# A recurrent kernel: the reset gate of one more step in eight summed over two halves, and one piece of work moved behind another

## The chip, the cores and the metric

The kernel runs on one core of one Trainium2 chip. The metric is the device time of one execution in microseconds. Before the change it is 1040.35 us, the median of three runs (1040.12 to 1040.90).

## The reference

64 sequences of 128 steps and 512 features go through a GRU whose first state is `cond_1024`; the result is added to x. After every fourth step, but not after the last, the state also goes through a propagation layer:

```python
comb = jnp.concatenate([x_t, h], axis=-1)
z = jax.nn.sigmoid(comb @ Wz + bz)
r = jax.nn.sigmoid(comb @ Wr + br)
comb2 = jnp.concatenate([x_t, r * h], axis=-1)
h_cand = jnp.tanh(comb2 @ Wh + bh)
h_new = (1.0 - z) * h + z * h_cand
h_next = jnp.where(prop, jnp.tanh(h_new @ Wp + bp), h_new)
```

All inputs are float32. Each step depends on the one before.

## The kernel before

**Layout.** Features lie on the 128 partitions in KC = 4 groups, the 64 sequences along the free dimension. The 128 steps are cut into 16 blocks of BLOCK = 8. `t` is the step, `m` its block and `s = t % 8` its place in the block. Every float32 operand of a matmul is split into two float16 parts, hi and lo, and a product is made of three of them: lo weights by hi values, hi by hi, hi weights by lo values.

**Two kinds of matmul.** The recurrent products (of h, of q = r*h, and of the state to propagate) have 64 columns. A *joint* product (`rec_both`, L1365 to L1371) multiplies the hi weights with the hi and lo values in one matmul of 128 columns; the two halves of the accumulator have to be added afterwards by VectorE (`tensor_reduce`, L1049 for R in two halves, L1067 for Z, L1084 for C), and the accumulator is opened (seeded) in both halves with half of the value (`seed`, L615). Steps 19 to 108 are joint for the update gate Z. The reset gate R is joint in them at places 0 to 6, not at place 7. The candidate C is joint at places 1, 4 and 6.

**The part of x.** The products of x with the input weights don't depend on h. They are made one or more blocks ahead and kept in `x_part`, from which the accumulators are seeded. For blocks 2 to 14 (`SEVEN`) the product of each gate is made of seven products of 2 x 2 quarters instead of eight: 21 *groups* a block, numbered 0 to 20 in `ORDER`, each 12 matmuls of 256 columns in one bank of PSUM. `STAGES_AT` says at which place TensorE makes which: at place 3 groups 7 and 8 ahead of the propagation and 9 behind it, at place 6 groups 15, 16 and 17, at place 7 groups 18 and 19 ahead of the propagation and 20 behind it. In a step with a joint R, the first four matmuls of the step's first group are put between Z and C (`AHEAD_OF_C`, L1413).

**Ends.** Most groups are read out by ScalarE (`read_stage`, L555). Products 5 and 6 of a gate (groups 4, 5, 11, 12, 17 and 19) are read by VectorE: `end_quarter` (L958 to L971) multiplies the bank and adds it to a quarter of `x_part` that ScalarE has begun. Group 17 is product 5 of the candidate, group 19 product 6. Before, the end of a group was issued in the step in which TensorE makes the group, the last thing of VectorE there but for the propagation. Group 20, product 7 of the candidate, goes into the bank of group 19, and so TensorE waits for its end:

```python
                elif product == 6:
                    pe.wait_ge(c12_begun, 2 * count)
                else:
                    pe.wait_ge(c22_out, count)
```

Group 9 (place 3) is product 3 of Z and waits for `first_copied` alone.

**The order of a step**, which is written out by hand for each engine. TensorE: R, Z (with the last of R's parts in between), the four matmuls ahead, C, then the groups of x, at places 3 and 7 the propagation between them. VectorE: R's reductions, q in hi (L1054) and in full (L1056), its lo part (L1032), Z's reduction (L1067), a split of x (L896), at joint candidates their reductions, keep (L1088), new (L1108), the state in hi (L1117), in full (L1120) and lo (L1032), at places 3 and 7 `add_states` for one step (L1127 by way of L1037), sums of quarters of x (L956), the ends (L969), and at places 3 and 7 the propagated state (L1147, L1150, L1032) and `add_states` for the other three. ScalarE: sigmoid of R, a split of x, squares, sigmoid of Z, tanh of C, the seeds of R and Z for the next step, the read-outs of x, the tanh of the propagation, the seed of C.

Of the kernel before, what the change touches and what calls it, by code (L numbers as in the profile page):

```python
# [16 lines left out]
BLOCK = 8  # L17
# [15 lines left out]
AHEAD = 32  # L33
REC_SUM_AT = 4
EARLY_PROP_SHARE = 1.4
JOINT_RESET_AT = (0, 1, 2, 3, 4, 5, 6)
AHEAD_OF_C = 4
JOINT = range(19, 109)
JOINT_CANDIDATE_AT = (1, 4, 6)
WITHIN_C = 4  # L40
SQUARES_AT = (0, 1, 2, 3)
# [7 lines left out]
SEVEN = range(2, 15)  # L49
# [4 lines left out]
ORDER = [(0, 1), (0, 2), (0, 3), (0, 4), (0, 5), (0, 6), (1, 1), (0, 7), (1, 2), (1, 3), (1, 4), (1, 5), (1, 6),  # L54
         (2, 1), (2, 2), (1, 7), (2, 3), (2, 5), (2, 4), (2, 6), (2, 7)]

STAGES_AT = [((), (0, 1)), ((), (2, 3, 4)), ((), (5, 6)), ((7, 8), (9,)), ((), (10, 11, 12)), ((), (13, 14)), ((), (15, 16, 17)), ((18, 19), (20,))]

SLOT_AT = {2: (5, 6, 6, 7, 8, 9, 10), 3: (4, 5, 6, 7, 7, 8, 9)}
SLOT_AT_LATER = (1, 2, 3, 4, 5, 6, 7)  # L60
# [8 lines left out]

def gru_kernel(nc, x, h0, wz, wr, wh, wp, biases, out):  # L70
    BLOCKS, _, KC, _, B = x.shape
    H = wp.shape[0]
    D = wr.shape[0] - H
# [22 lines left out]
    def in_tail(steps):  # L96

        if steps > len(TAIL_SHARES):
            return PER_GROUP * len(TAIL)
        shared = TAIL[:-KC]  # L100
        columns = [PER_GROUP * (of.stop - of.start) for _, _, of in shared]
        share, count = sum(columns) * sum(TAIL_SHARES[:max(steps, 0)]) / sum(TAIL_SHARES), 0
        for group in columns:
            count += min(int(max(share, 0) * PER_GROUP / group + 0.001), PER_GROUP)
            share -= group
        return count
# [30 lines left out]
    def stages_of(t):  # L137

        m, s = divmod(t, BLOCK)
        return STAGES_AT[s] if m + 1 in SEVEN else ((), ())  # L140

# [38 lines left out]
    with ExitStack() as ctx:  # L180
# [186 lines left out]
        def propagates(t):  # L367
            return t % CHUNK == CHUNK - 1 and t < T - 1

        def joint(t):  # L370

            return t in JOINT

        def behind_propagation(t):

            return propagates(t) and joint(t) and joint(t + 1)

        def joint_reset(t):

            return joint(t) and t % BLOCK in JOINT_RESET_AT  # L380

        def joint_candidate(t):

            return joint(t) and t % BLOCK in JOINT_CANDIDATE_AT

        def resets_before(t):
            return sum(joint_reset(step) for step in range(t))

        def candidates_before(t):
            return sum(joint_candidate(step) for step in range(t))  # L390

        def begun(t, n, stages):

            if n != stages[0] or not joint_reset(t):
                return 0
            return AHEAD_OF_C + (WITHIN_C if joint_candidate(t) else 0)
# [106 lines left out]
        def _(act):  # L503
# [81 lines left out]
            def squash_sums(g, func, summed, count, halves):  # L585

                for n, half in enumerate(halves):
                    act.wait_ge(summed, count + n + 1)
                    nc.scalar.activation(gate[g][:, half], gate[g][:, half], func, scale=unscale[:, g:g + 1]).then_inc(gate_ready[g], 1)  # L589
# [116 lines left out]
            for t in range(T):  # L706
# [25 lines left out]
                if joint(t):  # L732
                    squash_sums(Z, ACT.Sigmoid, update_summed, JOINT.index(t), WHOLE)
                else:
# [13 lines left out]
                if t + 1 < T and not ahead:  # L748
                    for g in (R, Z):
                        if g not in late and not (g == Z and behind_propagation(t)):  # L750
                            seed(g, t + 1)
# [10 lines left out]
                if propagates(t):  # L762
                    for n in range(first, middle):
                        copy_group(n)
                        seed_behind(n, late, t + 1)
                    for n in stages_first:
                        read_stage(m + 1, n)
                    act.wait_ge(squares_ready, KC + squares_before(t))
                    squash(PROP, ACT.Tanh, props_before(t), HALVES)
                    if behind_propagation(t):  # L770
                        seed(Z, t + 1)
                    for n in range(middle, last):
                        copy_group(n)
                        seed_behind(n, late, t + 1)
                    for n in stages_last:
                        read_stage(m + 1, n)
                else:
                    for n in range(first, last):
                        copy_group(n)
                        seed_behind(n, late, t + 1)  # L780
                    for n in stages_last:
                        read_stage(m + 1, n)
# [6 lines left out]
        def _(dve):  # L789
# [27 lines left out]
            def make_scale(col):  # L817

                one = slice(col, col + 1)
                dve.wait_ge(mag_reduced[col], 1)  # L820
                if col in ROOTS:
                    root_powers(pow2[:, one], scale[:, one], mag_sum(col), ROOTS[col], pow2_ready[col], 1, scale_ready[col])
                else:
                    powers(pow2[:, one], scale[:, one], mag_sum(col), pow2_ready[col], scale_ready[col])
                dve.wait_ge(pow2_ready[col], 1)
                if col < HS:
                    nc.vector.tensor_scalar(unscale[:, one], pow2[:, one], h_unscale, 0.5, ALU.mult, ALU.mult).then_inc(unscale_ready[col], 1)
                    dve.wait_ge(scale_ready[col], 1)
                    nc.vector.tensor_scalar(seed_scale[:, one], scale[:, one], h_scale, None, ALU.mult).then_inc(seed_scale_ready[col], 1)
                else:  # L830
                    nc.vector.tensor_scalar(unscale[:, one], pow2[:, one], 0.5, None, ALU.mult).then_inc(unscale_ready[col], 1)
                    if col > HS:
                        dve.wait_ge(unscale_ready[col], 1)
                        nc.vector.tensor_scalar(part_unscale[:, 0, col - WIN:col - WIN + 1], unscale[:, one], x_pow2[:, 0:1], 0.5,
                                                ALU.mult, ALU.mult).then_inc(part_unscale_ready, 1)
# [49 lines left out]
            def split_x(m, k, count=1):  # L885

                dve.wait_ge(x_scale_ready, m + 1)
                dve.wait_ge(x_hi_ready[m % 2], x_splits(m) - KC + k + count)
                nc.vector.scalar_tensor_tensor(out=x_lo[m % 2][:, k:k + count, :], in0=x_blk[m % RING][:, k:k + count].rearrange("p k s b -> p k (s b)"),  # L889
                                               scalar=x_scale[:, m % 2:m % 2 + 1], in1=x_hi[m % 2][:, k:k + count, :],  # L890
                                               op0=ALU.mult, op1=ALU.subtract).then_inc(x_lo_ready[m % 2], count)
# [66 lines left out]
            def end_quarter(m, n):  # L958

                g, product = ORDER[n]  # L960
                if product == 5:
                    dve.wait_ge(c12_begun, 2 * sevens(m, g))
                    bank, jh, done = BANK_C, 0, c12_out
                else:
                    dve.wait_ge(c22_begun, 2 * sevens(m, g))
                    bank, jh, done = BANK_A[g], 1, c22_out
                dve.wait_ge(seven_summed, len(ORDER) * (m - SEVEN.start) + n + 1)
                dve.wait_ge(part_unscale_ready, GATES + m)
                nc.vector.scalar_tensor_tensor(out=part_quarter(m, g, jh, 1), in0=in_halves(x_acc[bank][:]),  # L969
                                               scalar=part_unscale[:, m % 2, g:g + 1], in1=part_quarter(m, g, jh, 1),  # L970
                                               op0=ALU.mult, op1=ALU.add).then_inc(done, 1)  # L971
# [68 lines left out]
            for t in range(T):  # L1040
                m, s = divmod(t, BLOCK)
# [34 lines left out]
                if t == 1:  # L1076
                    make_scale(PROP)
                if t == JOINT[0] - 2:
                    nc.vector.tensor_scalar(half_seed_scale[:], seed_scale[:, R:C + 1], 0.5, None, ALU.mult).then_inc(half_seed_scale_ready, 1)
# [56 lines left out]
                if m + 2 == LAST:  # L1136
                    for k in SPLIT_AT.get(s, ()):
                        split_x(m + 2, k)
                for n in stages_of(t)[0] + stages_of(t)[1]:
                    if ORDER[n][1] in (5, 6):  # L1140
                        end_quarter(m + 1, n)
                if t in (1, 2):
                    split_rec(PROP, t - 1)
# [366 lines left out]
```

## Time and profile before

| | us |
|---|---|
| median of 3 runs | 1040.35 |
| the profiled execution | 1040.76 |
| its span | 1038.90 |
| TensorE busy | 1033.4 (99%) |
| VectorE busy | 880.9 (85%) |
| ScalarE busy | 777.0 (75%) |

The span runs from the first to the last instruction of the trace. PE is the matmuls of TensorE, PEld its weight loads, DVE is VectorE, ACT is ScalarE. Matmuls overlap: one of 64 columns is shown with 194 ns, though the next begins long before; what counts is the distance from start to start. The granted clock is full over the whole table of slices. `[0.16 <-DVE x_part L969]` behind an instruction says that its engine was idle for 0.16 us before it and that the named instruction released it; `issue` stands for no releaser that the trace shows.

### The profile page before, as it was taken

Reading aid. Unit: us, or ns where it says so; the run is one execution under the profiler, and the core shown is the slowest. Engines: PE = TensorE matmul, PEld = TensorE weight load, DVE = VectorE, ACT = ScalarE, POOL = GpSimd, SP = SyncE. Lnnn points to the kernel's source line nnn. Section 1 sums busy time; section 2 is a strip of 40 time slices with the busy share of each in tenths; the row PEclk is TensorE's granted clock in tenths of the full one; section 3 lists DMA queues with packets and bytes.
Section 4 is the critical chain, followed back from the end, with each engine's and each line's share of the span. In section 5 each row is a group of like instructions: output and inputs, shape, how many; then the busy total and the mean of one; then the engine's idle time right before and its main releaser. Section 6 shows DMA issues by size and latency. Waiting matters only on the chain.

```text
span 1038.9 us, 48087 instructions
## 1 busy us (share of the span) xinstructions
PE 1033.4 (99%) x20746; PEld 953.2 (92%) x20746; DVE 880.9 (85%) x2880; ACT 777.0 (75%) x1789; POOL 0.2 (0%) x4
## 2 busy tenths in 40 slices
PE   9999999999999999999999999999999999999998
PEld 4577999999999999999999999999999999999998
DVE  6978888898989899898989989989898998876666
ACT  6877777777878778777887777878777777665565
POOL 0000000000000000000000000000000000000000
PEclk9999999999999999999999999999999999999999
DMA  9312211001111011110011110111100100000001
GB/s 331 110 43 84 84 54 44 23 23 43 43 43 43 4 44 42 44 43 23 23 44 43 44 43 11 35 44 43 44 29 17 43 23 23 23 10 17 24 24 44
DMA packets 38484, 47.26 MB, mean 45 GB/s; under 512 B 2176, under 2 KB 34048, under 8 KB 37888
## 3 DMA queue, kind: packets, MB, share of 16 engines
q1 hardware_dynamic: 38000, 44.12, 12.6%
q8 instruction: 163, 2.67, 1.1%
q14 instruction: 49, 0.40, 0.1%
q10 hardware_dynamic: 272, 0.07, 0.0%
HBM read 27.40 MB, written 16.78 MB: 43 GB/s over the span
## 4 chain that ended last, share of the span: by engine, by line
PE 98%; DMA 1%; SPq 0%; DVE 0%; issue 0%; ACT 0%; DVEq 0%
PE acc L1360 38%; PE x_acc L1274 34%; PE acc L1368 17%; PE x_acc L1164 8%; DMA x_part<-wz_dram 1%; PE x_acc L1295 0%; SPq L419 0%; SPq L416 0%; DVE mag_win L982 0%; SPq L425 0%; SPq L424 0%; DVE x_lo L889 0%; PE acc L1170 0%; ACT gate L745 0%; DVE new L1099 0%
## 5 line engine op out<-in xcount | busy, mean ns | idle before, releaser
L1274 PE MATMUL x_acc<-x_hi,win_hi 128*128 128x256 f16 x1092 | 298.0, 273 | 0.0
L1274 PE MATMUL x_acc<-x_lo,win_hi 128*128 128x256 f16 x1092 | 297.9, 273 | 0.0
L1274 PE MATMUL x_acc<-x_hi,win_lo 128*128 128x256 f16 x1092 | 297.9, 273 | 0.0
L589 ACT ACTIVATE gate<-gate,unscale 128x128 f32<-128x128 f32 (+1 forms) x316 | 128.6, 432 | 136.4 <-DVE gate L1067 77.7
L595 ACT ACTIVATE gate<-acc,unscale 128x128 f32<-128x128 f32 (+1 forms) x384 | 123.8, 371 | 97.9 <-PE acc L1360 97.7
L1368 PE MATMUL acc<-h_split,wrec_hi 128*128 128x128 f16 x2704 | 178.8, 220 | 0.0
L1360 PE MATMUL acc<-h_split,wrec_lo 128*128 128x64 f16 x4096 | 177.5, 194 | 0.0
L1360 PE MATMUL acc<-q_split,wrec_hi 128*128 128x64 f16 x4000 | 162.2, 194 | 0.0
L555 ACT ACTIVATE x_part<-x_acc,bias,part_unscale 128x256 f32<-128x256 f32 x312 | 154.6, 561 | 6.4 <-PE x_acc L1274 5.5
L1360 PEld LDWEIGHTS acc<-h_split,wrec_lo 128*128 128x128 f16 x4096 | 154.2, 98 | 4.7
L1368 PEld LDWEIGHTS acc<-h_split,wrec_hi 128*128 128x128 f16 x2704 | 153.7, 98 | 0.0
L1360 PEld LDWEIGHTS acc<-q_split,wrec_hi 128*128 128x128 f16 x4000 | 136.5, 98 | 0.1
L617 ACT ACTIVATE acc<-x_part,half_seed_scale 128x512 f32<-128x512 f32 x203 | 135.3, 686 | 0.0
L1360 PE MATMUL acc<-q_split,wrec_lo 128*128 128x64 f16 x2544 | 120.8, 194 | 0.0
L1360 PE MATMUL acc<-h_split,wrec_hi 128*128 128x64 f16 x2784 | 117.6, 194 | 0.0
L1274 PEld LDWEIGHTS x_acc<-x_hi,win_lo 128*128 128x128 f16 x1092 | 106.8, 98 | 11.2
L1274 PEld LDWEIGHTS x_acc<-x_hi,win_hi 128*128 128x128 f16 x1092 | 106.8, 98 | 10.9 <-DVE x_part L969 0.2
L1274 PEld LDWEIGHTS x_acc<-x_lo,win_hi 128*128 128x128 f16 x1092 | 106.8, 98 | 10.0
L1360 PEld LDWEIGHTS acc<-q_split,wrec_lo 128*128 128x128 f16 x2544 | 98.6, 98 | 6.0 <-issue 0.5
L1360 PEld LDWEIGHTS acc<-h_split,wrec_hi 128*128 128x128 f16 x2784 | 96.4, 98 | 0.0
L1054 DVE TENSOR_TENSOR q_split<-gate,h_ring 128x128 f16<-128x128 f32 x192 | 54.8, 292 | 46.4 <-ACT gate L595 36.5
L626 ACT ACTIVATE acc<-x_part,seed_scale 128x256 f32<-128x256 f32 x180 | 83.0, 477 | 2.1 <-ACT x_part L522 0.4
(141 smaller groups left out, 1517.5 us busy)
## 6 DMA issues: line engine op xcount, KB each, us to landing
out_dram<-x_blk SPq DMA_DIRECT2D x30, 512.0 KB, 3.2
x_blk<-x_dram SPq DMA_DIRECT2D x24, 512.0 KB, 3.8
x_blk<-x_dram SPq DMA_DIRECT2D x3, 1024.0 KB, 8.7
x_part<-wz_dram SPq DMA_DIRECT2D x4, 256.0 KB, 6.8
x_part<-wh_dram SPq DMA_DIRECT2D x4, 256.0 KB, 6.6
x_part<-wr_dram SPq DMA_DIRECT2D x1, 1024.0 KB, 10.9
x_part<-wz_dram SPq DMA_DIRECT2D x1, 1024.0 KB, 13.1
x_part<-wh_dram SPq DMA_DIRECT2D x1, 1024.0 KB, 15.3
```

The lines of the kernel that those rows point to most:

```text
L555: nc.scalar.activation(part_quarter(m, g, jh, nh)[:, j], in_halves(x_acc[bank][:])[:, j], ACT.Identity, bias=bias[:, g, 2 * jh + j:2 * jh ...
L589: nc.scalar.activation(gate[g][:, half], gate[g][:, half], func, scale=unscale[:, g:g + 1]).then_inc(gate_ready[g], 1)
L595: nc.scalar.activation(gate[g][:, half, :], acc[g][:, half, :], func, scale=unscale[:, g:g + 1]).then_inc(gate_ready[g], 1)
L617: nc.scalar.activation(acc_bank[g][:], added.unsqueeze(1).broadcast_to([P, 2, KC, B]), ACT.Copy, scale=half_seed_scale[:, g:g + 1]).then_i ...
L626: nc.scalar.activation(acc[g], added, ACT.Copy, scale=seed_scale[:, g:g + 1]).then_inc(seed_ready[g], 1)
L1054: nc.vector.tensor_tensor(q_split[:, half, 0, :], gate[R][:, half, :], h_in[:, half, :], ALU.mult).then_inc(q_hi_ready, 1)
L1164: return nc.tensor.matmul(x_acc[bank][:, 0:cols], weights[g][:, 2 * (j // 2) + k // 2, k % 2, j % 2 * P:(j % 2 + 1) * P], values[m % 2][:, ...
L1274: mm = nc.tensor.matmul(in_halves(x_acc[bank][:])[:, j], weights[g][:, slot_w, k, j * P:(j + 1) * P], in_halves(values[m % 2][:, slot_x, : ...
L1360: mm = nc.tensor.matmul(bank[:, j, :], weights[g][:, k, j * P:(j + 1) * P], values[:, k, lo, :], start=False, stop=False, skip_group_check ...
L1368: mm = nc.tensor.matmul(acc_bank[g][:, :, j, :], wrec_hi[g][:, k, j * P:(j + 1) * P], values[:, k], start=False, stop=False, skip_group_ch ...
```

## The change

R becomes joint in all steps from 19 to 108, place 7 included (11 steps: 23, 31, ..., 103). With it come, in those steps: 16 matmuls of 128 columns in place of 32 of 64, two reductions on VectorE, a seed of both halves in the step before on ScalarE, and the first four matmuls of group 18 ahead of C. The conditions of C and of the seed behind the propagation are written anew and pick the same steps as before. The end of group 17 moves from place 6 to place 7, behind that of group 19, in all 13 blocks that make groups; the other ends stay where they were.

```diff
-JOINT_RESET_AT = (0, 1, 2, 3, 4, 5, 6)
 AHEAD_OF_C = 4
-JOINT = range(19, 109)
+JOINT_RESET = range(19, 109)
+JOINT = JOINT_RESET
...
+ENDS_AT = [(), (4,), (5,), (), (11, 12), (), (), (19, 17)]
...
         def behind_propagation(t):
 
-            return propagates(t) and joint(t) and joint(t + 1)
+            return propagates(t) and t + 1 in JOINT_RESET
 
         def joint_reset(t):
 
-            return joint(t) and t % BLOCK in JOINT_RESET_AT
+            return t in JOINT_RESET
 
         def joint_candidate(t):
 
-            return joint(t) and t % BLOCK in JOINT_CANDIDATE_AT
+            return t in JOINT_RESET and t % BLOCK in JOINT_CANDIDATE_AT
...
-                for n in stages_of(t)[0] + stages_of(t)[1]:
-                    if ORDER[n][1] in (5, 6):
+                if m + 1 in SEVEN:
+                    for n in ENDS_AT[s]:
                         end_quarter(m + 1, n)
```

## Rows read from the trace of the kernel before

**Rows 1.** The page: busy time of TensorE (part 1), chain that ended last (part 4).

```profile
PE 1033.4 (99%) x20746; PEld 953.2 (92%) x20746; DVE 880.9 (85%) x2880; ACT 777.0 (75%) x1789; POOL 0.2 (0%) x4
...
PE 98%; DMA 1%; SPq 0%; DVE 0%; issue 0%; ACT 0%; DVEq 0%
```

**Rows 2.** Windows, TensorE, the 11 steps of place 7: stretch, length, busy.

```profile
415.49:425.20 9.71, 9.67 (x215) 1.00 0.02 5
...
542.14:551.63 9.49, 9.49 (x215) 1.00 0.02 3
...
794.99:804.71 9.72, 9.72 (x215) 1.00 0.01 3
...
sum 104.83, PE 104.79; mean PE 9.53
```

**Rows 3.** Windows, TensorE, one step of place 3 (step 59).

```profile
509.93:519.38 9.45, 9.45 (x199) 1.00 0.01 2
```

**Rows 4.** Timeline, TensorE, start of that step: start, duration, instruction.

```profile
509.93 0.86 PE L1360 MATMUL acc<-h_split,wrec_lo 128*128 128x64 f16 x24
510.63 1.06 PE L1368 MATMUL acc<-h_split,wrec_hi 128*128 128x128 f16 x16
511.52 0.40 PE L1360 MATMUL acc<-h_split,wrec_lo 128*128 128x64 f16 x8
...
513.08 0.40 PE L1360 MATMUL acc<-q_split,wrec_lo 128*128 128x64 f16 x8
```

**Rows 5.** Timeline, TensorE, place 7 of the same block: the candidate begins.

```profile
544.90 0.40 PE L1360 MATMUL acc<-q_split,wrec_lo 128*128 128x64 f16 x8
```

**Rows 6.** Timeline, VectorE, the same step of place 7.

```profile
543.46 0.75 DVE L969 SCALAR_TENSOR_TENSOR x_part<-x_acc,part_unscale,x_part 128x512 f32<-128x512 f32 x1 [1.22 <-ACT x_part L555]
...
548.99 0.48 DVE L1037 SCALAR_TENSOR_TENSOR x_blk<-h_ring,unscale,x_blk 128x256 f32<-128x256 f32 x1
549.38 0.75 DVE L969 SCALAR_TENSOR_TENSOR x_part<-x_acc,part_unscale,x_part 128x512 f32<-128x512 f32 x1
550.98 0.54 DVE L1147 TENSOR_SCALAR h_split<-gate,scale 128x128 f16<-128x128 f32 x2 [0.85 <-ACT gate L595]
```

**Rows 7.** Timeline, VectorE, the step of place 3.

```profile
511.72 0.76 DVE L1049 TENSOR_REDUCE gate<-acc 128x128 f32<-128x256 f32 x2 [0.42 <-PE acc L1368]
...
517.30 0.48 DVE L1037 SCALAR_TENSOR_TENSOR x_blk<-h_ring,unscale,x_blk 128x256 f32<-128x256 f32 x1
517.70 0.69 DVE L956 TENSOR_TENSOR sum_b<-x_blk,sum_b 128x512 f32<-128x512 f32 x1
```

**Rows 8.** Timeline, VectorE, the step of place 7 from 415.49.

```profile
422.47 0.29 DVE L1032 TENSOR_TENSOR q_split<-h_ring,q_split 128x128 f16<-128x128 f32 x1 [0.25 <-issue]
...
423.08 0.74 DVE L969 SCALAR_TENSOR_TENSOR x_part<-x_acc,part_unscale,x_part 128x512 f32<-128x512 f32 x1
```

**Rows 9.** Timeline, weight loads of TensorE, the same step: group 20 begins.

```profile
423.87 0.10 PEld L1274 LDWEIGHTS x_acc<-x_hi,win_hi 128*128 128x128 f16 x1 [0.16 <-DVE x_part L969]
```

**Rows 10.** Timeline, VectorE, the step of place 7 from 794.99.

```profile
802.58 0.75 DVE L969 SCALAR_TENSOR_TENSOR x_part<-x_acc,part_unscale,x_part 128x512 f32<-128x512 f32 x1
```

**Rows 11.** The page's seeds (whole span), and ScalarE's timeline at places 7 and 3.

```profile
L617 ACT ACTIVATE acc<-x_part,half_seed_scale 128x512 f32<-128x512 f32 x203 | 135.3, 686 | 0.0
...
L626 ACT ACTIVATE acc<-x_part,seed_scale 128x256 f32<-128x256 f32 x180 | 83.0, 477 | 2.1 <-ACT x_part L522 0.4
...
543.32 0.48 ACT L626 ACTIVATE acc<-x_part,seed_scale 128x256 f32<-128x256 f32 x1
...
512.18 0.73 ACT L589 ACTIVATE gate<-gate,unscale 128x128 f32<-128x128 f32 x2 [1.09 <-DVE gate L1049]
```

**Rows 12.** Timeline, VectorE: two ends in a row (place 4's), and place 0.

```profile
274.33 1.40 DVE L969 SCALAR_TENSOR_TENSOR x_part<-x_acc,part_unscale,x_part 128x512 f32<-128x512 f32 x2
...
553.42 0.76 DVE L1049 TENSOR_REDUCE gate<-acc 128x128 f32<-128x256 f32 x2 [0.17 <-PE acc L1368]
```

**Rows 13.** Timeline, VectorE, step 111, behind the end of group 19.

```profile
930.95 0.54 DVE L1147 TENSOR_SCALAR h_split<-gate,scale 128x128 f16<-128x128 f32 x2 [1.05 <-ACT gate L595]
```

## The prediction

> **What bounds the kernel now.** I read the page first: its table of busy time and its chain of waits say the same thing, TensorE is busy for 99% of the span and the chain that ended last lies on it for 98% [rows 1]. So an edit is worth what it does to the time between TensorE's instructions, and nothing else. Next I took TensorE's busy time in stretches that are one time step each. Steps are called by their place in the block of 8 (step 23, 31, ..., 103 are the 11 steps of place 7 between 19 and 108, the only ones whose reset gate changes). Nine of the 11 take 9.49 us, two take 9.71 and 9.72, and all together 104.83 [rows 2]. A step of place 3 is built in the same way (it propagates too, and multiplies three groups of 12 for the next block), and its reset gate is already joint: the usual one takes 9.45 us, with 16 matmuls fewer [rows 3]. Place 3 is the model of what place 7 becomes.
>
> In the order of time, TensorE at place 3 goes from one group to the next without a gap, at 0.70 / 24 = 29 ns for a matmul of 64 columns and 0.89 / 16 = 56 ns for one of 128 [rows 4]. One joint matmul replaces two plain ones: 2 x 29.2 - 55.6 = about 2.5 ns each, 0.04 us for 16, which is 9.49 - 9.45. So TensorE gains next to nothing from joining: the columns stay, only instructions go.
>
> **What the joint reset gate does to VectorE.** Its own price is on VectorE and ScalarE: the two halves of the sum must be added before the sigmoid, so q is late, and with it everything behind q. At place 7 the candidate's first matmul begins 544.90 - 542.14 = 2.76 us into the step [rows 5, 2]; at place 3 it is 513.08 - 509.93 = 3.15 us [rows 4]. TensorE fills this with the first four matmuls of the step's first group (18, which the change now begins there), so it does not stop. VectorE has no such filling; from q on it runs its instructions one behind the other, and the delay is kept to the end. At place 7 it adds the step's result to x (L1037) at 548.99 - 542.14 = 6.85 us into the step and begins the end of quarter 19 (L969) at 7.24 [rows 6]; at place 3 the same L1037 begins at 517.30 - 509.93 = 7.37 and what is behind it at 7.77 [rows 7]. Place 7 gets the list of place 3 on VectorE up to that point (two reductions, q, its two parts, the update gate's reduction, one split of x, keep, new, the two forms of h, L1037), so the end of quarter 19 will begin at 7.77 instead of 7.24: 0.53 us later.
>
> **Who waits for it.** Product 7 of the candidate (group 20, the last of the step) goes into the bank that the end of quarter 19 reads, and TensorE waits for c22_out before it. Place 3 has no such wait: its last group, 9, needs only ScalarE's copy of group 6, made long before. The trace of before shows the wait at work once in a way that can be measured. In the step from 415.49 VectorE had an idle piece of 0.25 us that the trace puts down to nothing but issue, the end of quarter 19 began at 423.08, that is 7.59 into the step [rows 8], TensorE's weight load for group 20 came 0.16 us late with that very instruction as its releaser [rows 9], and the step ended at 425.20, 2.12 us after the beginning of the end of quarter 19. The second long step repeats it: 802.58 to 804.71 is 2.13 us [rows 10, 2]. In the nine other steps 7.24 + 2.12 = 9.36, which is 0.13 us ahead of 9.49: that is all the slack there is. The long step is late by 0.35 at the end of quarter 19 and by 0.22 at its own end, again 0.13 apart.
>
> So a step of place 7 after the change lasts 7.77 + 2.12 = 9.89 us. Eleven of them: 108.79, against 104.83 now. **The sum is +3.96 us.** Of this 9 x 0.40 = 3.6 come from the ordinary steps and 0.36 from the two long ones, which lose less because they are late already.
>
> **The rest of the change.** The end of quarter 17 leaves place 6, where VectorE waited for ScalarE's copy (L555) and only began at 543.46, 1.32 us into place 7 [rows 6]. Kept there with a joint gate, and later by the 0.21 of R's larger seed on ScalarE, it would free VectorE at 1.32 + 0.21 + 0.66 = 2.19, and the reductions are due at 511.72 - 509.93 = 1.79 [rows 7]: q would be late by 0.4. Moved, it holds up nothing there. Behind 19 it starts 0.66 us after it (two ends in a row take 1.40 together, one alone 0.74, so the second starts 0.66 behind the first [rows 12]), at 8.43, and the propagated state (L1147) follows at 9.09 instead of 550.98 - 542.14 = 8.84. Its first half is written 0.29 later, at 9.38. The next step begins at 9.89, so this is hidden by the wait before group 20; were that wait gone, 9.38 plus the passing of the semaphore would be at the step's very end (9.45) and could cost up to 0.1 us a step. VectorE is then free at 553.25 + 0.25, 11.36 into the step; its next reduction had 0.17 us of idle time [rows 12] and is itself moved on by 0.40, so nothing is passed on. Whoever waits for c12_out does so in the next block, several us later. Steps 15 and 111 get only the move: at 111 VectorE sat idle for 1.05 us before L1147 [rows 13], against 0.66 for one more end, so I take nothing for them (a loss of up to 0.1, no gain).
>
> ScalarE: the seed of R before place 7 becomes one of 512 elements, 686 ns instead of 477 [rows 11]. Its seed of C ends at 543.80, would end at about 544.03, 1.89 us into the step, and the joint sigmoid is due at 512.18 - 509.93 = 2.25 [rows 11]. Slack 0.36, cost nothing. If it were gone, q would be late and TensorE would stand before C.
>
> **Bounds.** The unknown in the sum is VectorE's pieces of 0.25 to 0.35 us of idle time without a releaser. In the steps of before two of 11 had one ahead of the end of quarter 19; there was then 0.13 us to take it, now there is none, so each costs its 0.35 in full. The change adds 22 reductions, so where they fall is open: none gives +3.96, one +4.3, two +4.6, four +5.4. Downwards: were the 0.04 us that each step saves on TensorE not met at all by the wait (all 11 steps at 9.45), the sum would be 103.95 - 104.83 = -0.9. I take one piece, as the count lies between none and two: +4.3, or 4.15 with the slight chance of none weighed in. The span of the profiled execution is 1038.90 of its 1040.76 us; the 1.86 around it stay. It lies 0.4 above the median of the runs, 1040.35, to which the difference is added: 1044.5.
>
> **The rivals.** (1) The wait is not felt, the other side: VectorE gets to the end of quarter 19 by 7.33 us into the step (9.45 - 2.12), the point from which it decides. Then the steps take 9.45 and the kernel 1040.35 - 0.9 = 1039.5, within 0.2% of before. For it speaks that TensorE at place 3 never stops; against it that place 3 has no group that waits for an end, and that every instruction between q and that end is already back to back. (2) The end of quarter 19 is early enough but 17 behind it delays h: up to 0.1 us in 11 steps less the 0.04 saved, 1041. It needs (1) first. (3) ScalarE is not free at 2.25: q late by, say, 0.5 (the seed's 0.21 and a piece of idle time), which adds to the end of quarter 19: 11 x 0.5 more, about 1050. The measured 0.36 speaks against it. (4) Loading weights sets TensorE's pace, and 16 loads fewer a step is the true gain: a load lasts 0.10 us [rows 9], 16 x 0.10 = 1.6 us a step, 17.6 in all, 1023. Against it: loads that follow at 29 ns each, and 9.49 against 9.45 with those 16 gone.
>
> The Trainium skill has a rule that speaks for (4): "TensorE: Matmul & The Clock Gate", sections "Back-to-back issue gap" and "LDWEIGHTS (loading the stationary operand)", says that in a stream of load and matmul the spacing is set by both, 81 ns at 128 columns, and that a load takes its columns over 1.2, 107 ns for 128. By 107 ns a load the change would save 16 x 107 x 11 = 18.8 us. The trace does not agree, with 56 ns at 128 columns and 29 at 64; it agrees with the formula that the page calls the isolated gap.
>
> **How the numbers follow.** Forecast 0.84; (1) 0.08, (2) 0.03, (3) 0.04, (4) 0.01. About 2.1 us (0.2%) is what a measurement of this kernel can tell from no change. The forecast and (3) are slower by more: 0.88. (1) and (2) are within: 0.11. (4) is faster: 0.01. The range for 8 in 10 holds the forecast with none to four pieces of idle time (1044.3 to 1045.7), and 0.9 below and 0.4 above for the small terms and for runs: 1043.4 to 1046.1.
>
> **What would show it.** In the profile after: TensorE's weight load of L1274 with L969 of VectorE as releaser in every step of place 7, about 0.4 us each; steps 23, 31, ... of 9.89 us; the end of quarter 19 at 7.77 into the step and 17 at 8.43; the candidate's first matmul at 3.15; the steps of place 0 to 6 unchanged (9.45 at place 3). It is wrong if place 7 takes 9.45 (rival 1), or if TensorE stops before the candidate's matmuls (rival 3).

## The result, and the profile after

Six runs of the changed kernel have a median of 1045.07 us (1044.3 to 1045.5), against 1040.7 for the kernel before beside them: a ratio of 1.0041, 95% interval 1.0029 to 1.0054. It is 4.4 us slower. The forecast was 1044.5, range 1043.4 to 1046.1.

The windows of TensorE over the 11 steps of place 7, stretch, length and busy time, which answer to [rows 2]. Three of the 11 rows of the kernel after, a usual one between the two long ones, and their sum:

```profile
416.78:426.80 10.02, 9.63 (x199) 1.00 0.02 5
...
544.14:554.03 9.89, 9.62 (x198) 1.00 0.01 2
...
862.35:872.49 10.14, 9.73 (x198) 1.00 0.02 4
sum 109.19, PE 105.98; mean PE 9.63
```

Nine steps take 9.89 or 9.90 us where nine took 9.49, and in each TensorE is shown idle for 0.27 us, which it was not before. (What it lost is more. The step would be 9.45 long without the stop, as experiment 8 shows, so the stop is 0.44. The shown gap is shorter, since a matmul of 64 columns is shown with 194 ns though the next can begin 29 ns behind it.) The sum is 4.36 above the 104.83 of before. The span grew by 4.5, from 1038.9 to 1043.4, so these 11 steps hold nearly all of it. The execution as a whole took 1045.23.

The same place as in [rows 6], in the step from 544.14, on VectorE (start, duration, instruction, idle time before it). The lines of the code are one higher than before (L970 is the end of a quarter, L1038 the addition to x, L1148 the propagated state):

```profile
545.93 0.75 DVE L1050 TENSOR_REDUCE gate<-acc 128x128 f32<-128x256 f32 x2 [1.69 <-PE acc L1369]
...
551.51 0.48 DVE L1038 SCALAR_TENSOR_TENSOR x_blk<-h_ring,unscale,x_blk 128x256 f32<-128x256 f32 x1
551.91 1.40 DVE L970 SCALAR_TENSOR_TENSOR x_part<-x_acc,part_unscale,x_part 128x512 f32<-128x512 f32 x2
553.23 0.47 DVE L1148 TENSOR_SCALAR h_split<-gate,scale 128x128 f16<-128x128 f32 x2
...
555.82 0.76 DVE L1050 TENSOR_REDUCE gate<-acc 128x128 f32<-128x256 f32 x2 [0.40 <-PE acc L1369]
```

TensorE in that step, where the candidate begins, and its weight load for group 20, which answers to [rows 9]:

```profile
547.30 0.40 PE L1361 MATMUL acc<-q_split,wrec_lo 128*128 128x64 f16 x8
```

```profile
552.71 0.10 PEld L1275 LDWEIGHTS x_acc<-x_hi,win_hi 128*128 128x128 f16 x1 [0.39 <-DVE x_part L970]
```

The waits of the changed kernel between 225 and 872.6 us (who waited for whom: us in total, times, longest) name the wait in all 11 steps. Before, the first of the two rows stood there once, with 0.2, and the second not at all:

```profile
PEld x_acc L1275 <- DVE x_part L970: 4.5, 11, 0.5
PE x_acc L1275 <- DVE x_part L970: 3.2, 11, 0.4
```

And the chain that ended last, part 4 of the page, which was 98% TensorE in [rows 1], now goes through VectorE:

```profile
PE 92%; DVE 6%; ACT 1%; issue 1%; DVEq 0%
```

6% of the span is some 60 us, while the loss is 4.4. In the step from 544.14 the chain leaves TensorE at the reductions (545.93) and comes back to it at the load for group 20 (552.71). So it counts all of VectorE's work that leads up to the late end, with two sigmoids of ScalarE, and most of it ran beside a busy TensorE. The share says where to look, the windows say how much.

### The profile page after: what moved, and what is told of

Its sections match the earlier page's. It is cut to its first block, busy times and chain, and to the rows that moved or that the text cites. A ratio compares the mean times of both kernels' runs of the same rounds, so it can differ in the third digit from the quotient of the medians.

```text
span 1043.4 us, 47768 instructions
## 1 busy us (share of the span) xinstructions
PE 1035.2 (99%) x20570; PEld 953.9 (91%) x20570; DVE 887.2 (85%) x2902; ACT 780.6 (75%) x1789; POOL 0.2 (0%) x4
## 4 chain that ended last, share of the span: by engine, by line
PE 92%; DVE 6%; ACT 1%; issue 1%; DVEq 0%
PE acc L1361 33%; PE x_acc L1275 32%; PE acc L1369 17%; PE x_acc L1165 8%; PE x_acc L1296 1%; ACT gate L590 1%; DVE q_split L1033 1%; DVE x_part L970 1%; DVE x_lo L897 1%; DVE gate L1068 1%; DVE q_split L1118 1%; DVE x_blk L1038 0%; DVE gate L1050 0%; DVE keep L1089 0%; DVE new L1109 0%
## 5 line engine op out<-in xcount | busy, mean ns | idle before, releaser
L590 ACT ACTIVATE gate<-gate,unscale 128x128 f32<-128x128 f32 (+1 forms) x338 | 136.6, 430 | 140.5 <-DVE gate L1068 78.1
L1369 PE MATMUL acc<-h_split,wrec_hi 128*128 128x128 f16 x2880 | 190.3, 219 | 0.0
L596 ACT ACTIVATE gate<-acc,unscale 128x128 f32<-128x128 f32 (+1 forms) x362 | 117.0, 372 | 90.0 <-PE acc L1361 90.0
L1361 PE MATMUL acc<-h_split,wrec_lo 128*128 128x64 f16 x4096 | 173.7, 193 | 0.0
L1369 PEld LDWEIGHTS acc<-h_split,wrec_hi 128*128 128x128 f16 x2880 | 163.7, 98 | 0.0
L618 ACT ACTIVATE acc<-x_part,half_seed_scale 128x512 f32<-128x512 f32 x214 | 142.1, 686 | 0.0
L1050 DVE TENSOR_REDUCE gate<-acc 128x128 f32<-128x256 f32 x180 | 68.0, 420 | 47.7 <-PE acc L1369 47.5
L1361 PE MATMUL acc<-h_split,wrec_hi 128*128 128x64 f16 x2432 | 101.8, 193 | 0.0
L1055 DVE TENSOR_TENSOR q_split<-gate,h_ring 128x128 f16<-128x128 f32 x192 | 55.1, 292 | 49.0 <-ACT gate L596 37.2
L1361 PEld LDWEIGHTS acc<-h_split,wrec_hi 128*128 128x128 f16 x2432 | 83.8, 98 | 0.0
```

Of the source, the lines that this page charges most:

```text
L596: nc.scalar.activation(gate[g][:, half, :], acc[g][:, half, :], func, scale=unscale[:, g:g + 1]).then_inc(gate_ready[g], 1)
L618: nc.scalar.activation(acc_bank[g][:], added.unsqueeze(1).broadcast_to([P, 2, KC, B]), ACT.Copy, scale=half_seed_scale[:, g:g + 1]).then_i ...
L1050: nc.vector.tensor_reduce(flat(gate[R][:, half]), acc_bank[R][:, :, half].rearrange("p n k b -> p (k b) n"), AX_X, ALU.add).then_inc(reset ...
L1055: nc.vector.tensor_tensor(q_split[:, half, 0, :], gate[R][:, half, :], h_in[:, half, :], ALU.mult).then_inc(q_hi_ready, 1)
L1361: mm = nc.tensor.matmul(bank[:, j, :], weights[g][:, k, j * P:(j + 1) * P], values[:, k, lo, :], start=False, stop=False, skip_group_check ...
L1369: mm = nc.tensor.matmul(acc_bank[g][:, :, j, :], wrec_hi[g][:, k, j * P:(j + 1) * P], values[:, k], start=False, stop=False, skip_group_ch ...
```

## The experiments

Each was timed beside the kernel before on the same chip, 2 and 3 with four runs, the others with ten or eleven. The ratio is to it. "Place 7" is the length of a usual one of the 11 steps in the profile, and the last column is the sum of the 11 (104.83 in the kernel before).

| kernel | R at place 7 | median us | ratio (95%) | place 7 | sum |
|---|---|---|---|---|---|
| after | joint | 1045.07 | 1.0041 (1.0029 to 1.0054) | 9.89 | 109.19 |
| 1: only the end of 17 moves | plain | 1039.79 | 0.9995 (0.9987 to 1.0004) | 9.49 | 104.39 |
| 2: only the gate changes | joint | 1049.61 | 1.0087 (1.0074 to 1.0101) | 10.30 | 113.63 |
| 3: 17 ahead of 19 | plain | 1046.73 | 1.0060 (1.0045 to 1.0076) | 10.02 | 110.26 |
| 4: 19 ahead of the addition | joint | 1040.97 | 1.0006 (0.9998 to 1.0015) | 9.51 | 105.03 |
| 5: the same | plain, 17 at place 6 | 1040.05 | 0.9998 (0.9989 to 1.0007) | 9.49 | 104.47 |
| 6: VectorE rearranged | joint | 1040.59 | 1.0004 (0.9995 to 1.0012) | 9.50 | 104.94 |
| 7: rearranged, split kept | joint | 1041.0 | 1.0006 (0.9997 to 1.0015) | 9.50 | 105.09 |
| 8: no end of 19 | joint | 1039.31 | 0.9987 (0.9978 to 0.9996) | 9.45 | 103.96 |
| 9: 1 and 5 together | plain | 1040.52 | 0.9997 (0.9988 to 1.0006) | 9.49 | 104.44 |

### 1. The move alone

```diff
         def joint_reset(t):
-            return t in JOINT_RESET
+            return t in JOINT_RESET and t % BLOCK != BLOCK - 1
```

> The kernel after, but with the plain reset gate at place 7: only the end of quarter 17 moves. Theory (the wait before group 20 for the end of quarter 19 is what costs): that end begins at 7.24 us into place 7 as before, so steps of place 7 take 9.49 us; 1040.7 us, ratio to before 1.000 within 0.001. Rival (the move itself costs, since 17 delays the propagated state): steps of place 7 above 9.6 us and a good part of the 4.3 us is there already.

```profile
sum 104.39, PE 104.39; mean PE 9.49
```

The move costs nothing that can be measured, and every one of the 11 steps takes 9.49. The two that were long are usual here too, because none of VectorE's pieces of idle time fell ahead of the end of 19 in this kernel: it begins at 7.25 in all 11. The theory holds, the rival falls.

### 2. The joint gate alone

```diff
-ENDS_AT = [(), (4,), (5,), (), (11, 12), (), (), (19, 17)]
+ENDS_AT = [(), (4,), (5,), (), (11, 12), (), (17,), (19,)]
```

> The kernel after, but with the end of quarter 17 back at place 6. Theory: that end begins at about 1.53 us into place 7 and frees VectorE at 2.19, the reductions of R start 0.4 late, TensorE stops 0.4 us before the candidate and the end of quarter 19 slips by 0.4 too: place 7 takes 10.29 us, 11 x 0.4 = 4.4 us over the kernel after: 1049.4. Rival (place 17 does not matter, only the wait before group 20 counts and has its own length): 9.89 us a step, 1045.1. Rival (both stops add up): 10.7 us a step, 1054.

VectorE in the step from 546.16:

```profile
547.70 0.75 DVE L970 SCALAR_TENSOR_TENSOR x_part<-x_acc,part_unscale,x_part 128x512 f32<-128x512 f32 x1 [1.44 <-ACT x_part L556]
548.37 0.74 DVE L1050 TENSOR_REDUCE gate<-acc 128x128 f32<-128x256 f32 x2
...
554.34 0.74 DVE L970 SCALAR_TENSOR_TENSOR x_part<-x_acc,part_unscale,x_part 128x512 f32<-128x512 f32 x1
```

TensorE's candidate in the same step:

```profile
549.69 0.39 PE L1361 MATMUL acc<-q_split,wrec_lo 128*128 128x64 f16 x8 [0.21 <-DVE q_split L1055]
```

The end of 17 begins 1.54 us into the step, the reductions at 2.21 instead of 1.79, the end of 19 at 8.18 instead of 7.77, and the step takes 10.30: 8.18 + 2.12. TensorE now stops twice. It stops 0.38 us before the candidate, which begins at 3.53 instead of 3.16 (its matmuls wait for L1055 in all 11 steps), and 0.47 before group 20, where the kernel after stops for 0.44. The lateness of q (0.40) is charged once: the first stop moves group 20 on nearly as far as the end of 19 slips, so the second stop hardly grows with it. One of the 11 steps took 10.61. A piece of idle time of VectorE in the step before it (0.25 us at 285.87) had made ScalarE's copies late, and with them the end of 17, by 0.32. 1049.4 was expected, 1049.6 measured. So the two parts of the change belong together: without the move the joint gate costs 9.2 us.

### 3. A late end without a joint gate

```diff
 (in kernel 1)
-ENDS_AT = [(), (4,), (5,), (), (11, 12), (), (), (19, 17)]
+ENDS_AT = [(), (4,), (5,), (), (11, 12), (), (), (17, 19)]
```

> The plain reset gate at place 7, and both ends there in the order 17, 19: the end of quarter 19 is late by 0.66 us without any joint gate. Theory: it begins at 7.90 into the step, group 20 waits, the step ends 2.12 later at 10.02; 9 x 0.53 + 2 x 0.31 in the steps from 23 to 103 and some 0.3 each at 15 and 111: +6.0, 1046.7. Rival (the cost of the change is in the joint gate, not in this wait): 9.49 us a step, 1040.7.

VectorE's two ends, 17 and then 19, in the step from 545.49:

```profile
552.74 1.40 DVE L970 SCALAR_TENSOR_TENSOR x_part<-x_acc,part_unscale,x_part 128x512 f32<-128x512 f32 x2
```

1046.73, and 10.02 a step. Kernel 1 differs from this one only in the order of these two instructions. The order costs 6.9 us against kernel 1 and 6.3 against the kernel before, more than the whole change did, with the gate plain. The end of 19 begins 7.91 us into the step (0.66 behind 552.74), and 7.91 + 2.12 is 10.03. It is the wait, whatever makes the end of 19 late. The 11 steps bring +5.4 of this, as expected. Steps 15 and 111 grew from 9.53 to 10.08 and 9.72, where about 0.3 had been expected of each.

### 4. The end of 19 ahead of the addition

```diff
+                end_first = joint_reset(t) and s == BLOCK - 1
+                if end_first:
+                    end_quarter(m + 1, 19)
                 if prop or t >= T - CHUNK:
                     dve.wait_ge(h_new_ready, 2 * t + 2)
                     add_states(t, t + 1)
```

(and 19 left out further down in these steps)

> The kernel after, with the end of quarter 19 ahead of the addition of the step's result to x in the 11 joint steps of place 7; the joint gate stays. Theory: the end begins at 7.37 instead of 7.77, the step takes 7.37 + 2.12 = 9.49 us; the kernel is 11 x 0.40 = 4.4 us faster than the kernel after less what pieces of idle time cost: 1040.7 to 1041.2. Rival (the joint gate costs by itself, through q or the propagated state): the step stays above 9.6 us and most of the 4.3 us stays.

The loss is gone but for 0.6 us, which the interval does not tell from nothing, with the joint gate in place. But the usual step takes 9.51, not 9.49, and place 0 behind it 6.777 instead of 6.765. VectorE in the step from 542.17:

```profile
549.55 0.74 DVE L970 SCALAR_TENSOR_TENSOR x_part<-x_acc,part_unscale,x_part 128x512 f32<-128x512 f32 x1
...
550.60 0.74 DVE L970 SCALAR_TENSOR_TENSOR x_part<-x_acc,part_unscale,x_part 128x512 f32<-128x512 f32 x1
551.26 0.47 DVE L1152 TENSOR_SCALAR h_split<-gate,scale 128x128 f16<-128x128 f32 x2
...
553.49 0.76 DVE L1050 TENSOR_REDUCE gate<-acc 128x128 f32<-128x256 f32 x2
```

The end of 19 begins at 7.38, but the propagated state only at 9.09 instead of 8.80, without idle time before it, since the end of 17 is still ahead of it. Its first half is there at 9.37 and the next step begins at 9.51. The reduction of the next step also has no idle time left before it. With the first wait down to 7.38 + 2.12 = 9.50, the second sets the step, at 9.51. So this is the prediction's rival 2 at work. From the beginning of the state to the next step are 0.42 us here, which would put the step 0.06 over 9.45 if the state alone were late; the prediction had said up to 0.1. That case was not run. What the late state adds to the wait is smaller, 0.02.

Two of the 11 steps are long here as well (9.63 and 9.77), and so are two in kernels 6 (9.62 and 9.86) and 7 (9.78 and 9.84): none of the three has slack for VectorE's pieces of idle time. In this one such a piece also fell into the late propagated state of step 55, at 488.79, and the step behind it took 7.13 instead of 6.78. The kernel after, whose next step begins later, has a piece at the same instruction too, and its place 0 stays at 6.77.

### 5 and 9. The same with the plain gate

Kernel 5 is the kernel before, kernel 9 is kernel 1, each with the lines of experiment 4 and `joint(t)` for `joint_reset(t)` in them.

> The kernel before (plain reset gate at place 7, 17 at place 6), with the end of quarter 19 ahead of the addition of one step's result in steps 23, 31, ..., 103. Theory: the end begins at 6.85 instead of 7.24 us into the step, the slack before group 20 grows from 0.13 to about 0.5 us, and VectorE's pieces of idle time no longer reach TensorE: all 11 steps at 9.49; 0.4 us less than before at most, ratio 0.9996, not to be told from 1. Rival (the two long steps of before are not from this wait): some steps stay above 9.6.

> The plain reset gate at place 7, the end of quarter 17 behind 19 as in the kernel after, and the end of 19 ahead of the addition of one step's result: everything that gives TensorE slack, nothing joint. Theory: 11 steps of 9.49 us, no long one; the same as the kernel with the move alone: 1039.8 to 1040.2, ratio 0.9997, not to be told from before. Rival (the slack is worth more, as some long steps in other places come from it): under 1039.3.

VectorE in the long step of kernel 9, from 415.54:

```profile
422.93 0.75 DVE L970 SCALAR_TENSOR_TENSOR x_part<-x_acc,part_unscale,x_part 128x512 f32<-128x512 f32 x1 [0.46 <-PE x_acc L1279]
```

Ten steps of each take 9.49, but neither expectation held in full. The end of 19 does not begin at 6.85 in kernel 5: it begins at 7.04 (548.76 - 541.72), since TensorE's last matmul of group 19 ends only at 6.94. So the slack before group 20 became 0.33 us and not 0.5. And a long step is left in each, which had been ruled out. In kernel 5 it takes 9.57: the piece lies between the two parts of q (798.23), and TensorE lost 0.08 us in the candidate, which needs them. (The second long step of the kernel before has its piece at the same place and lost the same 0.08 there; the wait before group 20 then made 0.22 of it.) In kernel 9 it takes 9.54: the end of 19 begins at 7.39 and not at 7.04, by which group 20 comes 0.02 us late, and the propagated state at 9.11, which with its 0.42 sets the step. Kernel 9 also has a median above the 1039.8 to 1040.2 that it was given. All of 1, 5 and 9 lie within 0.1% of before, and their intervals hold 1. In the profiles the slack is worth at most the 0.44 us of the two long steps, and that cannot be measured here.

### 6 and 7. VectorE's work at place 7 in another order

```diff
+                rearranged = joint_reset(t) and s == BLOCK - 1
+                if rearranged:
+                    add_states(t + 1 - CHUNK, t)
                 if joint_reset(t):
...
+                if not rearranged:
                     for block_m, slot in slots_at(t):
                         split_slot(block_m, slot)
...
-                if prop or t >= T - CHUNK:
+                if (prop or t >= T - CHUNK) and not rearranged:
...
-                    add_states(t + 1 - CHUNK, t)
+                    if rearranged:
+                        add_states(t, t + 1)
+                        for block_m, slot in slots_at(t):
+                            split_slot(block_m, slot)
+                    else:
+                        add_states(t + 1 - CHUNK, t)
```

(kernel 7 leaves `split_slot` where it was)

> The kernel after with VectorE's work at place 7 in another order in the 11 joint steps: the addition of three steps' results first (into the idle 1.7 us before the reductions), then as before but without the split of x, the ends of 19 and 17, the propagated state, the addition of one step's result and the split of x last. Theory: the end of quarter 19 begins as soon as TensorE has made group 19, at about 6.95, both ends are over by 8.3 and the propagated state begins at 8.80; TensorE never stops, 9.45 us a step as at place 3; 11 x 0.44 = 4.9 us under the kernel after, ratio to before 0.999. Rival (the joint gate has a cost of its own at place 7, or TensorE's 16 saved matmuls bring more than 0.04 us): a step above 9.5, or clearly under 9.45.

> As the rearranged kernel, but the split of x stays where it was, ahead of keep. Theory: the end of quarter 19 begins at 7.37 us (as with 19 ahead of the addition), group 20 begins at 7.37 + 0.81 = 8.18 instead of 8.14, and the propagated state is on time (8.80): 9.49 us a step, place 0 unchanged at 6.765. Rival (in the kernel with 19 ahead of the addition, the step's 9.51 came from the wait before group 20 and not from the late propagated state): 9.51 again.

Kernel 7's usual steps came out as expected: 9.50 and 6.765 at place 0, so the 9.51 and 6.777 of kernel 4 were the late state. Kernel 6 did not: 9.50 instead of 9.45, and a ratio of 1.0004 instead of 0.999. VectorE in its step from 541.73:

```profile
545.77 0.68 DVE L1071 TENSOR_REDUCE gate<-acc 128x256 f32<-128x512 f32 x1
547.03 0.43 DVE L1093 SCALAR_TENSOR_TENSOR keep<-gate,h_ring 128x256 f32<-128x256 f32 x1 [0.58 <-ACT gate L590]
...
549.11 1.40 DVE L970 SCALAR_TENSOR_TENSOR x_part<-x_acc,part_unscale,x_part 128x512 f32<-128x512 f32 x2
```

Without the split of x, VectorE waits 0.58 us for the sigmoid of Z, which needs VectorE's own reduction first. The split had filled that gap: taking 0.66 us of work out of a row of instructions brought 0. The end of 19 begins at 7.38 as in kernels 4 and 7, and 7.38 + 2.12 is 9.50. I had counted the instructions as one row that only VectorE sets, and had not asked what each was waiting for once its neighbour had gone.

### 8. Without the end of 19

```diff
-ENDS_AT = [(), (4,), (5,), (), (11, 12), (), (), (19, 17)]
+ENDS_AT = [(), (4,), (5,), (), (11, 12), (), (), (17,)]
...
-                else:
-                    pe.wait_ge(c22_out, count)
+                elif g != C:
+                    pe.wait_ge(c22_out, count - sevens(m, g) + 2 * (m - SEVEN.start) + g + 1)
```

(and ScalarE's wait for c22_out at place 4 likewise; the other two gates keep theirs, with the counts that are left)

This kernel leaves out a part of the result, and it serves only to measure.

> The kernel after with one thing left out: the end of quarter 19 (a quarter of the candidate's part of x stays without its last term) and the waits for it, in all 13 blocks. TensorE's matmuls are the same. Theory (that wait alone carries the cost): the end of quarter 17 begins at 7.77 us into place 7, the propagated state on time at 8.80, and all 11 steps take 9.45 as at place 3; 4.9 us under the kernel after, 0.9 under the kernel before in the profile, ratio to before 0.999. Rival (a late VectorE hurts by another way too, the candidate's start or the state): steps above 9.48, and part of the 4.3 us stays.

TensorE's windows over the steps of place 7:

```profile
226.28:235.73 9.45, 9.45 (x198) 1.00 0.01 2
...
sum 103.96, PE 103.96; mean PE 9.45
```

Every step takes 9.45 (the last 9.46), and VectorE has 0.29 us to spare before the propagated state, for the edit takes 0.66 us of its work away along with the wait. That the wait and not this work is what counts is seen from kernels 4 and 7, which keep the work and have 9.51 and 9.50. All the rest of the joint gate is still there: the reductions, the later q, the four matmuls ahead, the larger seed. So these cost TensorE nothing at place 7. Its 11 steps are together 0.9 us shorter than those of before, and it is the only kernel whose interval (0.9978 to 0.9996) lies below 1; it does less, so it is a measure of the wait and no rival to the others.

No version that computes everything beats the kernel before by more than can be measured. Kernel 1 has the lowest median of them, 0.6 us under the kernel before beside it, and its interval holds 1.

## Why the prediction was right

**TensorE's own gain.** Forecast 0.04 us a step from 16 fewer matmuls. Shown: 9.45 in experiment 8 against 9.49 in 1, same stretch, same order. (The prediction's own terms, 2 x 29.2 - 55.6, are 2.8 ns a pair and not 2.5; over 16 pairs that is 0.005 us.) Rival 4 (a load saved is 0.1 us saved) is dead.

**The candidate at 3.15 us.** It begins at 547.30 - 544.14 = 3.16 without a stop before it; rival 3 did not happen. That ScalarE and VectorE are free in time holds only because the end of 17 moved: in kernel 2 q is 0.40 late and TensorE stops for 0.38.

**The end of quarter 19 at 7.77.** It begins at 551.91 - 544.14 = 7.77, with all that VectorE does from q on back to back. Place 3 was a true model.

**2.12 us from there to the next step, 0.13 us of slack.** 554.03 - 551.91 = 2.12. The two long steps of the kernel before gave this number without an experiment; five kernels with four beginnings of that end confirm it (7.38 in 6 and 7, 7.77 in the kernel after, 7.91 in 3, 8.18 in 2, with steps of 9.50, 9.89, 10.03 and 10.30). Rival 1 falls with it: the end would have had to begin by 7.33, and it began at 7.77.

**The sum.** +3.96 with no piece of idle time, against +4.36 in these steps. The difference is two long ones, of 10.02 and 10.14: two pieces fell ahead of the end of 19. I had said 0.35 for each, in full. They cost 0.12 and 0.25. In the second, a piece of 0.16 stands in the trace at 866.42, between the parts of q, and the end of 19 begins at 8.02, 0.25 late. The delay is larger than the idle time shown, as 0.35 was for 0.25 in the kernel before, because instructions in a row overlap by about 0.09. In the first it is the new state's two parts (L1118) that take 0.60 instead of 0.49, too little for the trace to show as idle time, and the end of 19 begins at 7.89. That such pieces now reach TensorE in full is shown; their size was taken from two examples of one size and was too large, and their count, two where I took one, made up for it by luck. What causes them stays open.

**The propagated state at 9.09, hidden.** 553.23 - 544.14 = 9.09, and hidden as said; experiment 4 took the cover away and found it: 0.02 us over kernel 7, whose state is on time, and 0.012 in the step behind. VectorE's idle time before the next step's reductions is 0.40. I had 0.32: VectorE free at 11.36, and the reductions at 11.28 + 0.40 = 11.68, as they were.

**Steps 15 and 111, and the places around.** Both steps take 9.53 before and after, place 3 takes 9.45 and place 0 6.77 as before; kernel 1, with the same move at 15 and 111, is not slower than before.

## What to carry to other kernels

Where one engine is busy throughout, a change on another engine costs nothing until it uses up the slack of one particular wait, and then it costs all of the rest, and every small lateness that the slack used to take in comes on top; so look for the wait with the smallest slack behind the work that is delayed, and not for the busiest engine. A neighbouring stage that already has the new form, and a step that happened to be late in the trace of before, gave both numbers (how late, and what it costs) to 0.01 us. And an instruction that is issued in order behind others inherits their lateness: putting the one that someone waits for (the end of 19) ahead of the one that nobody waits for (the addition to x) took back most of the loss, while moving work that only filled a gap brought nothing.

## What was not expected of the hardware

VectorE has pieces of idle time with no releaser, which make it 0.1 to 0.35 us late, a handful in the 11 blocks. They come at other instructions when the program changes: in step 47 behind L1032 before (422.47) and within L1118 after, in step 95 before (798.64) and step 103 after (866.42). None fell ahead of the end of 19 at place 7 in kernel 1. Two instructions of VectorE in a row start closer than one lasts: the end of a quarter lasts 0.75 us and the next starts 0.66 after its beginning, so that 1.40 is the length of two. From the end's last moment to TensorE's weight load that waited for it there is 552.71 - (551.91 + 0.75) = 0.05 us.
